# A decoder's masked attention on one Trainium2 core: each penalty product of the scores as two products of 64 rows and columns

## What is computed

```python
q = query @ Wq.T + bq                       # query: layer norm of x;  16 heads of 8
k = key @ Wk.T + bk                         # key, values: ctx_1024
v = values @ Wv.T + bv
energy = jnp.einsum('bqhd,bkhd->bhqk', q, k) / math.sqrt(HEAD_DIM)
energy = jnp.where(mask == 0, jnp.float32(-10000000000.0), energy)
attn = jax.nn.softmax(energy, axis=-1)
out = jnp.einsum('bhqk,bkhd->bqhd', attn, v).reshape(b, sq, EMBED)
return out @ Wo.T + bo
```

## Time and profile before

| | before |
|---|---|
| median of 3 runs | 1168.65 us (1162.44 to 1185.16) |
| the profiled execution | 1171.92 us |
| its span, first to last instruction | 1170.1 us |
| PE busy | 1018.9 us (87%) |
| DVE busy | 901.3 us (77%) |
| ACT busy | 677.5 us (58%) |
| POOL busy | 628.0 us (54%) |
| mean granted clock of PE | 0.947 |

### The profile page before, as it was taken

How to read it: one execution, slowest core, us unless ns; L and a number is a source line. 1 busy time by engine, 2 the same in 40 slices (tenths; PEclk the granted TensorE clock), 3 DMA queues, 4 the chain that set the end, 5 groups by cost and what they waited for, 6 DMA issues and landing times.

```text
span 1170.1 us, 33353 instructions
## 1 busy us (share of the span) xinstructions
PE 1018.9 (87%) x10238; PEld 706.7 (60%) x10238; DVE 901.3 (77%) x2462; ACT 677.5 (58%) x1737; POOL 628.0 (54%) x956
## 2 busy tenths in 40 slices
PE   3799999999989887999877867978999999877997
PEld 2466666666657776777655646754555555555775
DVE  5588899888895796888867867764777777748896
ACT  1377787777776433554435546752566665646775
POOL 8667778876773445433344453157556751423554
PEclk9999999999996698999989989996999999979999
DMA  5765578966672001333321101015554551044550
GB/s 145 171 141 125 123 153 171 186 140 137 150 186 77 21 35 64 108 100 91 90 57 34 30 22 54 1 30 121 121 109 104 118 115 30 2 166 176 180 179 28
DMA packets 81442, 119.66 MB, mean 102 GB/s; under 512 B 16704, under 2 KB 62688, under 8 KB 80272
## 3 DMA queue, kind: packets, MB, share of 16 engines
q1 hardware_dynamic: 66688, 85.24, 30.5%
q0 software_dynamic: 9472, 27.27, 7.8%
q10 hardware_dynamic: 5136, 5.31, 2.3%
HBM read 80.75 MB, written 36.18 MB: 100 GB/s over the span
## 4 chain that ended last, share of the span: by engine, by line
PE 44%; DVE 17%; issue 15%; DMA 14%; POOL 6%; ACT 2%; SPq 1%; DVEq 1%; POOLq 0%; ACTq 0%
DMA experts_gathered<-experts_y_dram,experts_index 6%; PE heads_ps_pv L987 4%; PE heads_ps_max L965 4%; PE cross_ps_max L965 4%; DVE heads_neg_max L769 3%; PE cross_ps_pv L987 3%; DMA experts_xs_dram<-QK,experts_index 3%; PE cross_ps_max L955 3%; PE cross_ps_exp L958 2%; DMA QK<-heads_qk_parts 2%; DVE experts_hidden L1739 2%; PE experts_ps_gu L2451 2%; PE heads_ps_out L1049 2%; POOL experts_xs_dram L2142 1%; PE heads_ps_pv L1036 1%
## 5 line engine op out<-in xcount | busy, mean ns | idle before, releaser
L769 DVE TENSOR_REDUCE heads_neg_max<-heads_ps_max 128x4 f32<-128x512 f32 x256 | 169.3, 681 | 34.6 <-PE heads_ps_max L965 32.7
L843 ACT ACTIVATE heads_E<-heads_ps_exp 128x512 f32<-128x512 f32 x256 | 150.2, 604 | 22.4 <-PE heads_ps_pv L987 17.7
L769 DVE TENSOR_REDUCE cross_neg_max<-cross_ps_max 128x4 f32<-128x512 f32 x128 | 86.9, 686 | 49.6 <-PE cross_ps_max L965 48.9
L2156 POOL DMA_INDIRECT experts_gathered<-experts_y_dram,experts_index x64 | 61.8, 966 | 99.5 <-issue 69.9
L965 PE MATMUL heads_ps_max<-QK 48*128 48x128 bf16 x1024 | 102.1, 224 | 10.4 <-DMA QK<-heads_qk_parts 6.6
L969 PE MATMUL heads_ps_exp<-QK 50*128 50x128 bf16 x1024 | 103.0, 222 | 0.0
L2379 ACT ACTIVATE experts_act_out<-experts_ps_gu 128x256 f32<-128x256 f32 x110 | 42.3, 385 | 100.1 <-PE experts_ps_gu L2453 99.4
L843 ACT ACTIVATE cross_E<-cross_ps_exp 128x512 f32<-128x512 f32 x128 | 76.6, 599 | 40.5 <-PE cross_ps_exp L969 22.1
L2142 POOL DMA_INDIRECT experts_xs_dram<-QK,experts_index x64 | 61.5, 962 | 68.3 <-DMA experts_xs_dram<-QK,experts_index 52.6
L965 PEld LDWEIGHTS heads_ps_max<-QK 48*128 48x128 bf16 x1024 | 58.4, 96 | 51.6 <-issue 19.2
L987 PE MATMUL heads_ps_pv<-heads_E,heads_V 128*32 128x128 f32 x2048 | 84.9, 285 | 0.0
(11 more groups left out here) (323 smaller groups left out, 3238.4 us busy)
## 6 DMA issues: line engine op xcount, KB each, us to landing
experts_share<-experts_cT_dram SPq DMA_DIRECT2D x7, 2304.0 KB, 8.5
heads_qk_parts<-heads_parts POOLq DMA_DIRECT2D x32, 384.0 KB, 4.7
QK<-heads_qk_parts SPq DMA_DIRECT2D x64, 192.0 KB
QK<-heads_qk_parts SPq DMA_DIRECT2D x64, 128.0 KB
cross_qk_parts<-cross_parts POOLq DMA_DIRECT2D x16, 384.0 KB, 4.3
QK<-cross_qk_parts SPq DMA_DIRECT2D x32, 192.0 KB
experts_xs_dram<-load_stats SPq DMA_DIRECT2D x26, 192.0 KB, 2.9
experts_xs<-experts_xs_dram SPq DMA_DIRECT2D x78, 64.0 KB
```

The lines of the kernel that those rows point to most:

```text
L769: nc.vector.tensor_reduce(neg_max[:, half, heads.start:heads.stop], ps_max[:, u % 2, :].rearrange("q (h k) -> q h k", h=HU), AX.X, ALU.max ...
L843: nc.scalar.activation(E[:, half, heads.start:heads.stop, :], ps_exp[:, u % 2, :].rearrange("k (h q) -> k h q", h=HU), ACT.Exp, scale=scal ...
L2156: pool.indirect_dma_start(gathered[n % GATHERS][:], None, y_dram[h], bass.IndirectOffsetOnAxis(index[:, choice, b:b + 1], 0)).then_inc(loa ...
```

## The change

Each penalty product becomes two, over quarters of the array. The identity is diagonal, so only its two diagonal blocks of 64 x 64 do anything. The one for max uses rows and columns 0 to 63 (r = 0) and 64 to 127 (r = 1). The one for exp reads rows 0 to 63 and writes partitions 64 to 127, and the other way round; for that the transposed mask is loaded with its halves exchanged, in two transfers. The order of the four is max r = 0, exp r = 0, max r = 1, exp r = 1. Each still moves 512 columns.

```diff
@@ -510,7 +510,7 @@
-        LOADS = 4 + 2 * masked
+        LOADS = 4 + 3 * masked
@@ -587,7 +587,8 @@
                 sp.dma_start(mask_in[:, 0, :], mask[0]).then_inc(loaded[0], 16)
-                sp.dma_start(mask_in[:, 1, :], mask[1]).then_inc(loaded[0], 16)
+                for r in range(2):
+                    sp.dma_start(mask_in[r * BASE:(r + 1) * BASE, 1, :], mask[1][(1 - r) * BASE:(2 - r) * BASE, :]).then_inc(loaded[0], 16)
@@ -951,12 +952,14 @@
-                if masked and with_max:
-                    nc.tensor.matmul(ps_max[:, u % 2, :].rearrange("q (h k) -> q h k", h=HU), identb[:],
-                                     drop_q[:].unsqueeze(1).to_broadcast([S, HU, S]), start=True, stop=False, skip_group_check=True)
-                if masked and with_exp:
-                    nc.tensor.matmul(ps_exp[:, u % 2, :].rearrange("k (h q) -> k h q", h=HU), identb[:],
-                                     drop_k[:].unsqueeze(1).to_broadcast([S, HU, S]), start=True, stop=False, skip_group_check=True)
+                for r in range(2):
+                    here, there = slice(r * BASE, (r + 1) * BASE), slice((1 - r) * BASE, (2 - r) * BASE)
+                    if masked and with_max:
+                        nc.tensor.matmul(ps_max[here, u % 2, :].rearrange("q (h k) -> q h k", h=HU), identb[here, here],
+                                         drop_q[here].unsqueeze(1).to_broadcast([BASE, HU, S]), start=True, stop=False, skip_group_check=True)
+                    if masked and with_exp:
+                        nc.tensor.matmul(ps_exp[there, u % 2, :].rearrange("k (h q) -> k h q", h=HU), identb[here, here],
+                                         drop_k[here].unsqueeze(1).to_broadcast([BASE, HU, S]), start=True, stop=False, skip_group_check=True)
```

## The result

| | before | changed |
|---|---|---|
| median of 20 runs | 1176.96 us | 1165.2 us |
| lowest to highest | 1162.44 to 1199.43 | 1155.95 to 1182.74 |
| span of the profiled execution | 1170.1 us | 1161.7 us |
| first score for max to last score for exp | 213.8 us | 203.2 us |

The changed kernel takes 0.9923 of the time of before, with a 95% interval from 0.9894 to 0.9951: faster by 9 us, between 6 and 12. A few executions of each kernel are over 1.5% slower than its fastest and do not count in this ratio; the medians in the table are of all 20, and differ by 11.8. The three runs of before that the forecast had to go by had a median of 1168.65; with 20 it is 1176.96. The forecast, 1158 against 1168.65, is a ratio of 0.991; on the longer series it would read 1166.

A forecast was written before the change was run, and what follows sets the result against it. PE was taken to bound the mixed steps until DVE is in the way. Terms -24.0 + 10.4 + 2.2 + 1.0 gave -10.4 us, 1161.5 by the profile, stated as 1158 by the median; own range 1154 to 1163, wider 1145 to 1172.

The forecast's parts named there:

- the last term: Whole kernel: the median of three runs lies 3.3 us below the profile, turning 1161.5 us into 1158.
- the clock at the start of the mixed steps: Masked attention: the clock not rising at 820, or falling in the mixed steps, was given 2% and no cost.
- Part 1: Penalties in mixed steps: four quarters run at once, saving 0.20 us a unit, together -24.0 us.
- Part 2: Mixed steps: three more changes of array shape a step, 0.12 us each over 29 steps, +10.4 us.
- Part 3: Three max-only and three exp-only steps: no overlap saving, 18 added passages at 0.12 us, +2.2 us.
- Part 4: Unit u0, PE's transpose waiting for DVE's shift: its saving mostly lost in some 15 of 29 steps, +1.0 us.
- A: Penalties: the passage between quarters and halves is free, -21.5 us, 1150 by profile or 1147 by median; 10%.
- B: Penalties: two row halves cannot write one bank at once, +20.3 us, 1192 or 1189 by median; 13%.
- C: Penalties: column halves overlap badly, three rounds a unit, +38 us with passages, 1210 or 1207; 5%.
- D: Exp-only steps: the clock falls early, near 999, 8 us counted lost, net -2, 1169 or 1166; 10%.

The follow-up runs named there:

- e8: The kernel before, unchanged, profiled a second time; first score for max to last for exp 221.2 us, exp-only part 27.8 us.
- e6: Changed kernel with each penalty as one product of 64 rows and 128 columns, half the mask left out; masked stretch 186.7 us against 203.2.
- e4: Changed kernel with quarters only in units 1 to 3 and whole products in unit 0; ratio 0.9895 to the kernel before, masked stretch 202.7 us.
- e7: Changed kernel with the four quarters reordered to max, max, exp, exp; masked stretch 202.6 us against 203.2.
- e5: Kernel before without any penalty in the 29 mixed steps, that part of the mask left out; masked stretch 179.1 us against 213.8.

## Why the prediction was right and where it failed

The sum had -10.4 us. The stretch lost 10.3 in the first profile; over the profiles, without e8 and its fallen clock, 212.3 on the mean of two before and 202.4 on the mean of three changed, 9.9; the runs say 9 (6 to 12). The direction, the place and the size of the gain held; the time did not. 1165.2 is 7.2 us above the 1158, and above the forecast's own range of 1154 to 1163, though inside the wider one from 1145 to 1172. Two steps failed.

The first is the last term, "the median of the three runs lies 3.3 us lower": it took the median of three executions, 23 us apart, for that of the kernel. Over 20 the median of before lies 5.0 us above the profiled execution and not 3.3 below: 8.3 us, more than the whole miss.

The second is in the mechanism: the clock at the start of the mixed steps, put at nothing and 2%, gave back some 3 us. That the sum still met the stretch's 10.3 is luck in part: this loss was left out and part 1 saved a little less than summed, and against that parts 2, 3 and 4 had their costs too high.

- **Part 1, the products overlap: right.** 0.53 us to the first score became 0.34: 0.19 a unit, where 0.20 was summed, 1 to 2 us too much in 112. The starts lie within 0.01 us.
- **Part 2, one more passage: right in number and price.** It shows ahead of u0, u2 and u3 as 0.09 to 0.10 (L1046 to the penalty 0.20 for 0.11, L999 0.31 for 0.22) and not ahead of u1, and e6 has 0.11 for the one behind the penalties. With 0.12 I was high by some 2 us in 87. Parts 1 and 2 together: 12.5 to 12.6 us in 27 steps at the full clock, 13.5 in 29; the sum had 24.0 - 10.4 = 13.6. Most steps went from 6.09 and 6.25 to 5.62 and 5.78 us. Four came down to 5.88 and no further; three around 900 came down from 6.29.
- **Part 3, the steps with one kind alone: half.** The exp-only part grew from 19.3 to 20.1, where 9 x 0.12 = 1.1 was summed. The max-only part did not grow: 19.2 and 17.8 before (19.9 in e8), 18.9, 18.2 and 19.2 changed. Spells of the higher clock within it are larger than a microsecond.
- **Part 4, DVE at u0: over-sized.** +1.0 was summed. e4 shows that u0's 0.09 is lost in four steps, 0.4 us. The forecast sets 846 beside 902 as "one step further on", but they are nine steps apart, and small and large margins alternate in part of the stretch only: in the kernel before the margin is 0.05 to 0.06 us in each of the seven steps from 902. In the changed kernel it is 0.05 to 0.14 in 22 of 32 steps, and yet behind the first mixed step PE stands idle at none of the L1033, where a wait at every other one had been forecast. A small margin is not a wait. The one wait that there is, 0.27 us at the lower clock, the forecast did not have.
- **What the sum left out: the clock at the start.** "That the clock would not rise at 820 ... I put at 2%." It rose 8.8 to 11.3 us after the first score for exp in all five profiles with quarters there, and at most 4.9 after in the three of before. The mixed part became 163.6 on the mean of three, 10.6 less than the 174.2 of before, though its steps save 13.6: 3 us were given back in the first three or four steps, the wait of 0.27 among them. I had reasoned from a stretch where the clock stays up without penalties (100 to 200 in the earlier trace rows); what holds a clock up says little of what raises it.
- **The rivals.** A is out by e6, B by e7, C by the starts and by the 0.34, where three rounds would take 0.65. D, an early fall at the end, did not come with quarters; it came once in the kernel before.

The Trainium skill, TensorEngine Tiling (Array Packing), Tiling Modes, Key Properties (a change of mode drains the engine): the 0.11 of e6 agrees for quarters to halves, the 0.09 ahead of the penalties for the whole array to quarters. The sentence of its Gotcha 1: PSUM Pressure, that different row tiles cannot access one bank simultaneously, does not hold as it stands: e7's pair for max writes one bank from both halves of the rows, each its own 64 partitions, at once. Whether it holds for the same partitions was not tried.

## What to carry to other kernels

A product with an identity is mostly zeros: only its diagonal blocks need the array, and blocks of two such products can run in each other's empty corners, at the price of one passage of 0.09 to 0.11 us wherever the array changes its shape. Count the passages on both sides of the work before splitting it, and put the split first where the neighbour has another shape already (0.19 us a unit in u1, 0.09 in the others here). A median of three executions that lie 23 us apart is no base for a forecast of 10 us. And compare the stretch that the change touches, not whole executions, when something ahead of it varies by more than the gain.

## What the runs showed of the hardware that was not expected

- A PE that is busy nearly all the time was not enough for the full clock. It stood at 1.2 GHz for 18 us of max-only steps with PE busy for 17.8 of them. Where penalties were whole in at least three units, it was up at the latest 5.3 us after the exp scores had joined on the other half of the rows, in one profile before they did, but 8.8 to 11.3 us after where all were in quarters, which also had a wait of 0.26 us there.
- In e5, without penalties, it fell amid the mixed steps, behind 3 us in which PE was busy for 1.7; and in one execution of the kernel before it fell 20 us earlier than in two others, which alone cost 8.5 us.
- Four products of 64 rows and 64 columns start 3 to 4 ns apart by the trace (within 0.01 us in the rows), and the next work starts 0.34 us behind the first of them, where behind one whole product it is 0.31.
